# Tokens in another column order through all stages, with x1 and y stored row by row

## The chip, the cores and the metric

The kernel runs on one core of one Trainium2 chip. The metric is the device time of one execution in microseconds; less is better. Engines are named as in the profile: PE (TensorE matmuls), PEld (its weight loads), DVE (VectorE), ACT (ScalarE), POOL (GpSimd) and SP (SyncE, which here only issues DMAs). A DMA is split into pieces that are contiguous on both sides; the profile counts them as packets.

## What is computed

The input x is an image of 512 by 512 tokens with 128 channels, in fp32. Two layers follow one another, each added to its input. `_gn` normalises groups of 4 channels over the whole image.

```python
# layer 0: x = x + L0(_gn(x))
a = sigmoid((x @ Wa1 + ba1) * (x @ Wa2 + ba2))        # 16 channels
b = sigmoid((x @ Wb1 + bb1) * (x @ Wb2 + bb2))
g = sigmoid(x @ Wg + bg)
z = einsum('bikc,bkjc->bijc', a, b)
return g * (_ln(z) @ Wz + bz)
# layer 1: x = x + L1(_gn(x))
xn = layernorm(x)
h = linear(xn, pi) * sigmoid(linear(xn, gi)) * mask[..., None]
a1, b1, a2, b2 = split(h, 4, axis=-1)                 # 32 channels each
x1 = einsum('bikd,bjkd->bijd', a1, b1)
x2 = einsum('bkid,bkjd->bijd', a2, b2)
yn = layernorm(concatenate([x1, x2]))
return linear(yn, po) * sigmoid(linear(yn, go))
```

## The kernel before

The program has seven stages with a barrier between them. Tensors go through DRAM from one to the next: a_d, b_d, z_d, x1_d, h_d, y_d, r_d. Every engine's order is written out by hand with semaphores; no scheduler is at work.

- **Stage 1** (to 430 us) reads x in pieces of 64 KB and gathers statistics.
- **Stage 2** (`stage2_gates`, 430 to 1250 us) reads x in 256 loads of 8 rows by 128 columns (line 341: 128 partitions, one per column, 8 pieces of 512 B each), transposes to channels on partitions (line 353), projects and stores a_d and b_d in blocks of 128 tokens. A load waits for the slot to be transposed; there are four slots.
- **Stage 3** (`stage3_triangle`, to 1713 us) makes 16 channels of z for 128 rows at a time and stores z_d, channel by row by column, in four DMAs of 4 MB from POOL's queue (line 597).
- **Stage 4** (`stage4_layer0`, 1713 to 2640 us) goes row by row through the image, 16 rows to a loop pass in four groups of four. For a row, PE transposes four blocks of 128 tokens (line 680), multiplies z (line 688) and the gate (line 690), ACT makes the sigmoid (line 716), DVE mixes (line 749), POOL adds (line 783). SP's queue does for each group, in this order: the store of four rows of x1 (line 649, 1 MB), two loads of x (line 640, 512 KB each) and two of z (line 644, the same 32 channels to two places). x1_d has the channel as its first dimension, so a partition's four rows are one piece of 8 KB and partitions are 1 MB apart. x is read with `(i q p) c -> p i q c`: partition p takes the tokens p, 128+p, 256+p and 384+p of a row, four pieces of 512 B.
- **Stage 5** (`stage5_project`, to 4785 us) works on 16 regions of 128 by 128 tokens of x1_d, read in pieces of 512 B, and stores h_d. The mask comes into mask_n with one DMA (line 841); PE turns it (line 1066) and DVE keeps it (line 961) before the first tokens.
- **Stage 6** (`stage6_triangles`, to 5517 us) makes the 64 channels of y, each from 48 products (line 1196), and stores one channel of y_d at a time, 1 MB, from POOL's queue (line 1240). y_d has the channel first, so this megabyte is contiguous. Its last steps store r_d, the scale of each token.
- **Stage 7** (`stage7_layer1`, 5517 to 6609 us) goes through rows again. SP loads for four rows y (two DMAs of 64 partitions, line 1339) and r_d (line 1341), and for two rows x1 (line 1343). PE spreads the scale (line 1355), DVE scales (line 1403), ACT rounds (line 1449), DVE makes the rest (line 1407), PE projects (lines 1359 to 1361), ACT makes the gate (line 1454), DVE mixes (line 1413), POOL adds x1 (line 1484), PE transposes back (line 1375), ACT copies out (line 1438) and issues the store of two rows (line 1442), in pieces of 512 B.

Which token of a row stands in which column is free as long as all stages agree, since the products sum over all tokens of a row or column.

## Time and profile before

| | us |
|---|---|
| median of 3 runs | 6601.09 |
| lowest and highest | 6581.02, 6617.51 |
| profiled execution | 6610.76 |
| span of its instructions | 6609.1 |
| PE / DVE / ACT / POOL busy | 5324.7 / 4933.3 / 3568.5 / 2397.8 |

The span is the time from the first to the last instruction. The mean granted TensorE clock is 0.929 of full speed. The 16 DMA engines moved 1521.58 MB, 230 GB/s in the mean; 1461952 of the 1673897 packets are under 2 KB. Shares of the whole span mix stages with different limits, so what follows is read stage by stage.

### The profile page before, as it was taken

The numbers are of one execution on the slowest core, as the hardware profiler recorded it, in microseconds if no ns is written. First come the engines' busy times: TensorE is split into PE (matmuls) and PEld (weight loads), VectorE is DVE, ScalarE is ACT, GpSimd is POOL, SyncE is SP. The second block draws the span as 40 slices with busy tenths as digits, with TensorE's granted clock in tenths as the row PEclk, the third lists the DMA queues.
The fourth block names the chain that finished last, engine by engine and source line by source line (L and its number), as shares of the span: only waits on it lengthen the run. The fifth ranks groups of instructions, "written<-read, shape, count | busy, mean of one in ns | idle before, by whom it ended". The sixth has DMA issues, their size and how long they took to land. (4 is left out here: it accounts for less than half of the span.)

```text
span 6609.1 us, 113036 instructions
## 1 busy us (share of the span) xinstructions
PE 5324.7 (81%) x31445; PEld 3093.9 (47%) x31445; DVE 4933.3 (75%) x8646; ACT 3568.5 (54%) x5390; POOL 2397.8 (36%) x1756
## 2 busy tenths in 40 slices
PE   0026766755588888899999999999899996999999
PEld 0025655522355554555555555555544443445454
DVE  6887877465777778677777777777778886777776
ACT  0037888522566666444434443444367774777776
POOL 0014444200477776223322332333200003656665
PEclk9998888877799999899989998999899998999999
DMA  8967777765799999454455445544588886999999
GB/s 306 369 224 204 211 204 208 254 236 209 225 337 327 329 335 302 111 138 118 118 140 137 118 118 141 135 118 118 153 316 303 303 277 203 310 311 316 313 319 297
DMA packets 1673897, 1521.58 MB, mean 230 GB/s; under 512 B 42752, under 2 KB 1461952, under 8 KB 1655232
## 3 DMA queue, kind: packets, MB, share of 16 engines
q1 hardware_dynamic: 1319536, 1265.61, 62.2%
q10 hardware_dynamic: 332288, 167.79, 8.9%
q0 software_dynamic: 21840, 85.46, 3.2%
q8 instruction: 98, 1.61, 0.1%
q14 instruction: 135, 1.11, 0.1%
HBM read 997.04 MB, written 521.67 MB: 230 GB/s over the span
## 5 line engine op out<-in xcount | busy, mean ns | idle before, releaser
L915 ACT ACTIVATE s_gate<-s_g_ps,k_gi_bias 128x512 f32<-128x512 f32 x512 | 351.7, 687 | 1059.8 <-PE s_g_ps L1103 1059.8
L927 POOL TENSOR_TENSOR s_rstd<-s_var,k_minus_half 128x16 f32<-128x16 f32 x130 | 377.1, 2901 | 1495.1 <-DVE s_var L983 1495.1
L1484 POOL TENSOR_TENSOR s_oT<-s_gated,s_x1t 128x512 f32<-128x512 f32 x512 | 650.6, 1271 | 442.1 <-DVE s_gated L1413 435.7
L783 POOL TENSOR_TENSOR s_x1T<-s_gz,s_xT 128x512 f32<-128x512 f32 x512 | 650.0, 1269 | 254.4 <-DVE s_gz L749 252.8
L1196 PE MATMUL s_y_ps<-s_ab 128*128 128x512 f16 x3072 | 665.0, 380 | 36.0 <-DVE s_ab L1259 36.0
L395 POOL TENSOR_TENSOR s_low<-s_xh,s_high 128x512 f16<-128x512 f32 x256 | 383.4, 1498 | 849.0 <-DVE s_high L391 849.0
L1103 PE MATMUL s_g_ps<-s_xc,k_Wgi 128*128 128x512 f32 x1024 | 593.7, 662 | 0.0
L1005 DVE TENSOR_TENSOR s_xc<-s_xh,s_rstd_ps 128x512 f32<-128x512 f32 x513 | 352.6, 687 | 265.5 <-PE s_rstd_ps L1097 215.5
L749 DVE SCALAR_TENSOR_TENSOR s_gz<-s_z_ps,k_z_bias,s_g 128x512 f32<-128x512 f32 x512 | 384.5, 751 | 213.0 <-ACT s_g L716 210.7
L1106 PE MATMUL s_p_ps<-s_xc,k_Wpi 128*128 128x512 f32 x1024 | 535.7, 605 | 0.0
L690 PE MATMUL s_g_ps<-s_xT,s_Wg 128*128 128x512 f32 x1024 | 523.6, 593 | 0.0
L1012 DVE SCALAR_TENSOR_TENSOR s_h<-s_p_ps,k_pi_bias,s_gate 128x512 f32<-128x512 f32 x512 | 384.0, 750 | 152.7 <-PE s_p_ps L1106 149.0
L1196 PEld LDWEIGHTS s_y_ps<-s_ab 128*128 128x128 f16 x3072 | 301.0, 98 | 399.7 <-issue 38.6
L1454 ACT ACTIVATE s_gate<-s_g_ps,k_go_bias 128x512 f32<-128x512 f32 x512 | 352.0, 687 | 228.0 <-PE s_g_ps L1361 219.9
L969 DVE BATCH_NORM_STATS2 s_stats<-s_x_ps 128x6 f32<-128x128 f32 x2080 | 469.0, 283 | 5.4 <-PE s_x_ps L1083 5.4
L716 ACT ACTIVATE s_g<-s_g_ps,s_bg 128x512 f32<-128x512 f32 x512 | 351.8, 687 | 192.2 <-PE s_g_ps L690 192.2
L680 PEld LDWEIGHTS s_x_ps<-k_ident,s_xt 128*128 128x128 f32 x2048 | 247.3, 142 | 408.9 <-issue 241.4
L893 ACT ACTIVATE s_xh<-s_xg,k_gn_shift,k_gn_scale 128x512 f32<-128x512 f32 x524 | 420.5, 804 | 24.7 <-DMA s_xg<-x_d 24.5
L1407 DVE TENSOR_TENSOR s_low<-s_yn,s_high 128x512 f16<-128x512 f32 x256 | 267.5, 1045 | 222.9 <-ACT s_high L1449 222.9
L680 PE MATMUL s_x_ps<-k_ident,s_xt 128*128 128x128 f32 x2048 | 315.3, 277 | 103.7 <-DMA s_xt<-in_x 97.2
L412 ACT ACTIVATE s_xh<-s_turned_ps,k_gn_shift,k_gn_scale 128x512 f32<-128x512 f32 x512 | 373.7, 783 | 39.1 <-PE s_turned_ps L353 33.6
L364 PE MATMUL s_proj_ps<-k_Wab_high,s_high 128*128 128x64 f16 x2048 | 243.9, 197 | 180.4 <-DVE s_pre L481 172.6
(209 smaller groups left out, 12723.1 us busy)
## 6 DMA issues: line engine op xcount, KB each, us to landing
s_xt<-in_x SPq DMA_DIRECT2D x512, 512.0 KB, 6.6
s_xg<-x_d SPq DMA_DIRECT2D x264, 512.0 KB, 5.7
x_d<-s_x1T SPq DMA_DIRECT2D x128, 1024.0 KB, 6.3
h_d<-s_out SPq DMA_DIRECT2D x128, 1024.0 KB, 8.1
s_x1t<-x_d SPq DMA_DIRECT2D x256, 512.0 KB, 6.7
out<-s_ot ACTq DMA_DIRECT2D x256, 512.0 KB, 7.5
s_bt<-b_d SPq DMA_DIRECT2D x64, 1024.0 KB, 7.8
s_at<-h_d SPq DMA_DIRECT2D x64, 1024.0 KB, 4.9
```

The lines of the kernel that those rows point to most:

```text
L395: engine.tensor_tensor(low[:, u % 8, :], xh[:, u % 4, :], high[:, u % 8, :], ALU.subtract).then_inc(rest_ready[u % 2], 1)
L680: last = pe.transpose(x_ps[:, i % 4, q * P:(q + 1) * P], xt[:, i // U, i % U, q, :], K.ident[:])
L690: pe.matmul(g_ps[:, i % 2, 0:N], Wg[:], xT[:, i % 8, :], start=True, stop=True).then_inc(g_prod, 1)
L749: dve.scalar_tensor_tensor(gz[:, i % 4, :], z_ps[:, i % 2, 0:N], K.z_bias[:], g[:, i % 2, :], ALU.add, ALU.mult).then_inc(mixed, 1)
L783: pool.tensor_tensor(x1T[:, i // U, i % U, :], gz[:, i % 4, :], xT[:, i % 8, :], ALU.add).then_inc(added, 1)
L893: act.activation(xh[:, unit // 4 % 4, 4 * (unit % 4):4 * (unit % 4) + 4, :], src, ACT.Identity, bias=K.gn_shift[:], scale=K.gn_scale[:]).t ...
L969: last = dve.bn_stats(stats[:, 4 * (unit % 4) + r, :], x_ps[:, unit % 2, r * P:(r + 1) * P])
L1012: dve.scalar_tensor_tensor(h[:, 4 * unit:4 * unit + 4, :].rearrange("p r j -> p (r j)"), p_ps[:, unit % 2, :], K.pi_bias[:], gate[:, unit ...
L1103: pe.matmul(g_ps[:], K.Wgi[:], xc[:, unit % 2, :], start=True, stop=True).then_inc(g_done, 1)
L1106: pe.matmul(p_ps[:, unit % 2, :], K.Wpi[:], xc[:, unit % 2, :], start=True, stop=True).then_inc(p_done, 1)
L1196: last = pe.matmul(y_ps[:, n % 8, 0:N], ab[:, u % 2, 0, a, kb, ib * P:(ib + 1) * P], ab[:, u % 2, 1, b, kb, :], start=m == 0, stop=m == le ...
L1484: pool.tensor_tensor(oT[:, row % 4, :], gated[:, row % 2, :], x1t[:, row // 2, row % 2, :], ALU.add).then_inc(added, 1)
```

## The change

The column order changes from `(q p)` to `(p q)`: block q of a row now holds the tokens 4p+q, so the four tokens of a partition are neighbours, 2 KB in x and in the output. Rows go into blocks the same way (i = 4m+b) where a block of 128 rows is on the partitions: stage 2 reads rows 4 apart, stages 3 and 6 store their 128 rows 4 apart, stage 5 reads them so. x1_d becomes row by channel by column and y_d likewise, so one row of x1 is 256 KB in one piece and one channel of y is spread over the whole of y_d. Pieces: x loads of stage 4 and output stores of stage 7 from 512 B to 2 KB; x1 stores from 8 KB to 2 KB; x1 loads of stage 7 from 4 KB to 2 KB; the others keep their size. The mask is loaded into the tile h first, and one copy on DVE puts its columns in the new order. Stage 7 loads y with one DMA instead of two.

```diff
--- before.py
+++ after.py
@@ -304,7 +304,7 @@
     ROWS, UNITS = 8, 64
     PAIRS = UNITS // 2
     LAG = 4
-    x_v = x.rearrange("(rb n r j) c -> rb n j r c", rb=RB, r=ROWS, j=N)
+    x_v = x.rearrange("(n r b p q) c -> b q n p r c", r=ROWS, b=RB, p=P, q=RB)
     with ExitStack() as stack:
         s = Scope(nc, stack, "s2")
         xt = s.sbuf("xt", [P, 4, ROWS, P])
@@ -337,7 +337,7 @@
                         for n in range(32):
 
                             sp.wait_ge(turned, r * UNITS + (2 * n + 2))
-                            src = x_v[bass.ds(rb, 1), n % 16, bass.ds((c2 * 2 + n // 16) * P, P)].rearrange("a j r c -> (a j) r c")
+                            src = x_v[bass.ds(rb, 1), bass.ds(c2 * 2 + n // 16, 1), n % 16].rearrange("a e p r c -> (a e p) r c")
                             sp.dma_start(xt[:, n % 4, :, :], src).then_inc(loaded[n % 4], 16)
 
             @block.tensor
@@ -500,6 +500,7 @@
 
 
     RB, C, SLOTS = N // P, 16, 4
+    z_v = z_d.rearrange("c (p b) j -> b p c j", b=RB)
     with ExitStack() as stack:
         s = Scope(nc, stack, "s3")
         at = s.sbuf("at", [P, SLOTS, RB, P])
@@ -594,7 +595,7 @@
                 pool.sem_inc(left, 1)
                 with pool.Fori(0, RB) as ib:
                     pool.wait_ge(z_split, ib * 2 + 2)
-                    pool.dma_start(z_d[:, bass.ds(ib * P, P), :].rearrange("c i j -> i c j"),
+                    pool.dma_start(z_v[bass.ds(ib, 1)].rearrange("a p c j -> (a p) c j"),
                                    parts[:].rearrange("p h c j -> p (h c) j")).then_inc(stored, 16)
                     pool.wait_ge(stored, ib * 16 + 16)
                     pool.sem_inc(left, 1)
@@ -606,7 +607,7 @@
 
     CB, ROWS, U = N // P, 16, 4
     GROUPS = ROWS // U
-    x_v = x.rearrange("(i q p) c -> p i q c", q=CB, p=P)
+    x_v = x.rearrange("(i p q) c -> p i q c", q=CB, p=P)
     with ExitStack() as stack:
         s = Scope(nc, stack, "s4")
         xt = s.sbuf("xt", [P, GROUPS, U, CB, P])
@@ -646,7 +647,7 @@
                 def group(r, n, last=False):
 
                     sp.wait_ge(added, r * ROWS + (U * n + U + 8))
-                    sp.dma_start(x1_d[:, bass.ds(r * ROWS + U * n, U), :], x1T[:, n, :, :]).then_inc(stored[n], 16)
+                    sp.dma_start(x1_d[bass.ds(r * ROWS + U * n, U)].rearrange("i p j -> p i j"), x1T[:, n, :, :]).then_inc(stored[n], 16)
                     if not last:
                         sp.wait_ge(turned, r * ROWS + (U * n + U))
                         load_x(r + 1, n)
@@ -794,6 +795,7 @@
 
     RB, GROUPS = N // P, 8
     last_region = RB * RB
+    x1_v = x1_d.rearrange("(m b) p j -> b p m j", b=RB)
     with ExitStack() as stack:
         s = Scope(nc, stack, "s5")
         xg = s.sbuf("xg", [P, 2, 8, P])
@@ -802,6 +804,7 @@
         gate = s.sbuf("gate", [P, 2, BANK])
         h = s.sbuf("h", [P, P, P])
         rows_out = s.sbuf("rows_out", [P, 2, BANK])
+        mask_raw = h[:, 0:RB * N // P, :].rearrange("m (b k) c -> m b (k c)", b=RB)
         out1 = s.sbuf("out1", [P, 64, P])
         out2 = s.sbuf("out2", [P, 64, P])
         mask_n = s.sbuf("mask_n", [P, RB, N])
@@ -822,7 +825,7 @@
             return (t_ps if n % 4 < 2 else p_ps)[:, n % 2, :]
 
         loaded = s.sems("loaded", 2)
-        mask_loaded, mask_turned, mask_kept = [s.sem(n) for n in ("mask_loaded", "mask_turned", "mask_kept")]
+        mask_loaded, mask_parted, mask_turned, mask_kept = [s.sem(n) for n in ("mask_loaded", "mask_parted", "mask_turned", "mask_kept")]
         normed, x_turned, counted, var_ready, rstd_ready, parts_ready, parts_turned, rows_ready, chain = [
             s.sem(n) for n in ("normed", "x_turned", "counted", "var_ready", "rstd_ready", "parts_ready", "parts_turned", "rows_ready", "chain")]
 
@@ -838,13 +841,13 @@
         def _(block):
             @block.sync
             def _(sp):
-                sp.dma_start(mask_n[:], mask.rearrange("(b p) j -> p b j", p=P)).then_inc(mask_loaded, 16)
+                sp.dma_start(mask_raw, mask.rearrange("(p b) j -> p b j", b=RB)).then_inc(mask_loaded, 16)
 
                 def load(g, n):
 
                     place = g % last_region
                     sp.wait_ge(normed, g * 32 + (2 * n + 1))
-                    src = x1_d[:, bass.ds(place // RB * P + 8 * n, 8), bass.ds(place % RB * P, P)]
+                    src = x1_v[bass.ds(place // RB, 1), :, 8 * n:8 * n + 8, bass.ds(place % RB * P, P)].rearrange("a p m j -> (a p) m j")
                     sp.dma_start(xg[:, n % 2, :, :], src).then_inc(loaded[n % 2], 16)
 
                 def store(g, t, out, part):
@@ -952,6 +955,10 @@
 
             @block.vector
             def _(dve):
+                dve.wait_ge(mask_loaded, 16)
+                dve.tensor_copy(mask_n[:].rearrange("m b (q p) -> m b p q", q=RB),
+                                mask_raw.rearrange("m b (p q) -> m b p q", q=RB)).then_inc(mask_parted, 1)
+                dve.wait_ge(mask_parted, 1)
                 dve.sem_inc(scaled, 16)
                 dve.sem_inc(counted, 2)
                 dve.sem_inc(h_ready, 2)
@@ -1058,7 +1065,7 @@
             def _(pe):
                 pe.sem_inc(h_turned, 32)
 
-                pe.wait_ge(mask_loaded, 16)
+                pe.wait_ge(mask_parted, 1)
                 for cb in range(RB):
                     if cb >= 2:
                         pe.wait_ge(mask_kept, cb - 1)
@@ -1157,6 +1164,7 @@
 
 
     RB, D, SLOTS = N // P, 64, 4
+    y_v = y_d.rearrange("(p b) d j -> d p b j", b=RB)
     with ExitStack() as stack:
         s = Scope(nc, stack, "s6")
         at, bt = s.sbuf("at", [P, SLOTS, RB, N]), s.sbuf("bt", [P, SLOTS, RB, N])
@@ -1237,12 +1245,12 @@
                 with pool.Fori(0, D // GROUP) as r:
                     for u in range(GROUP):
                         pool.wait_ge(copied, r * (GROUP * RB) + ((u + 1) * RB + 8))
-                        pool.dma_start(y_d[bass.ds(r * GROUP + u, 1)].rearrange("a (b p) j -> p (a b) j", p=P),
+                        pool.dma_start(y_v[bass.ds(r * GROUP + u, 1)].rearrange("a p b j -> (a p) b j"),
                                        y[:, u, :, :]).then_inc(stored, 16)
                         pool.wait_ge(stored, r * (GROUP * 16) + (u + 1) * 16)
                         pool.sem_inc(left, 1)
                 pool.wait_ge(parts_ready, 1)
-                pool.dma_start(r_d.rearrange("(b p) k j -> p b k j", p=P), parts[:]).then_inc(parts_stored, 16)
+                pool.dma_start(r_d.rearrange("(p b) k j -> p b k j", b=RB), parts[:]).then_inc(parts_stored, 16)
                 pool.wait_ge(parts_stored, 16)
 
             @block.vector
@@ -1303,9 +1311,9 @@
 
 
     CB, PAIRS = N // P, 4
-    y_v = y_d.rearrange("d (r e) j -> e d r j", e=2)
+    y_v = y_d.rearrange("(r e) d j -> (e d) r j", e=2)
     r_v = r_d.rearrange("(r e) k j -> (e k) r j", e=2)
-    out_v = out.rearrange("(i q p) c -> p i q c", q=CB, p=P)
+    out_v = out.rearrange("(i p q) c -> p i q c", q=CB, p=P)
     with ExitStack() as stack:
         s = Scope(nc, stack, "s7")
         yt = s.sbuf("yt", [P, 2, 2, N])
@@ -1335,12 +1343,10 @@
                     for n in range(PAIRS):
                         if n % 2 == 0:
                             sp.wait_ge(scaled, r * PAIRS + (n + 2))
-                            for e in range(2):
-                                sp.dma_start(yt[64 * e:64 * e + 64, n // 2, :, :],
-                                             y_v[e, :, bass.ds(r * PAIRS + n, 2), :]).then_inc(y_loaded[n // 2], 16)
+                            sp.dma_start(yt[:, n // 2, :, :], y_v[:, bass.ds(r * PAIRS + n, 2), :]).then_inc(y_loaded[n // 2], 16)
                             sp.dma_start(rt[:, n // 2, :, :], r_v[:, bass.ds(r * PAIRS + n, 2), :]).then_inc(y_loaded[n // 2], 16)
                         sp.wait_ge(added, r * ROWS + (2 * n + 2))
-                        sp.dma_start(x1t[:, n, :, :], x1_d[:, bass.ds(r * ROWS + 2 * n, 2), :]).then_inc(x_loaded[n], 16)
+                        sp.dma_start(x1t[:, n, :, :], x1_d[bass.ds(r * ROWS + 2 * n, 2)].rearrange("i p j -> p i j")).then_inc(x_loaded[n], 16)
 
             @block.tensor
             def _(pe):
@@ -1350,7 +1356,7 @@
                 def spread_scale(r, n):
                     r, n = r + n // PAIRS, n % PAIRS
                     if n % 2 == 0:
-                        pe.wait_ge(y_loaded[n // 2], r * 48 + 48)
+                        pe.wait_ge(y_loaded[n // 2], r * 32 + 32)
                     pe.wait_ge(scaled, r * PAIRS + (n + 4))
                     pe.matmul(r_ps[:, 0:N], K.halves[:], rt[:, n // 2, n % 2, :], start=True, stop=True).then_inc(spread, 1)
 
@@ -1496,9 +1502,9 @@
     a_d = nc.dram_tensor("a_d", [RB, P, 16, N], FP32, kind="Internal").ap()
     b_d = nc.dram_tensor("b_d", [RB, P, 16, N], FP32, kind="Internal").ap()
     z_d = nc.dram_tensor("z_d", [32, N, N], FP16, kind="Internal").ap()
-    x1_d = nc.dram_tensor("x1_d", [P, N, N], FP32, kind="Internal").ap()
+    x1_d = nc.dram_tensor("x1_d", [N, P, N], FP32, kind="Internal").ap()
     h_d = nc.dram_tensor("h_d", [2, RB, P, 64, N], FP32, kind="Internal").ap()
-    y_d = nc.dram_tensor("y_d", [64, N, N], FP32, kind="Internal").ap()
+    y_d = nc.dram_tensor("y_d", [N, 64, N], FP32, kind="Internal").ap()
     r_d = nc.dram_tensor("r_d", [N, 3, N], BF16, kind="Internal").ap()
     with ExitStack() as stack:
         s = Scope(nc, stack, "k")
```

On SyncE's queue, at the end of a pass of stage 7 (four rows), before:

```order
L1339 ISA [waits s7_scaled]
L1339 DMA s_yt<-y_d 64x2x512
L1339 ISA
L1339 DMA s_yt<-y_d 64x2x512
L1341 ISA
L1341 DMA s_rt<-r_d 6x2x512
L1342 ISA
L1343 ISA [waits s7_added]
L1343 DMA s_x1t<-x_d 128x1024
```

and with the change:

```order
L1346 ISA [waits s7_scaled]
L1346 DMA s_yt<-y_d 128x2x512
L1347 ISA
L1347 DMA s_rt<-r_d 6x2x512
L1348 ISA
L1349 ISA [waits s7_added]
L1349 DMA s_x1t<-x_d 128x2x512
```

One of the two y loads ahead of r_d is gone, and the x1 load has two runs of 512 elements to a partition in place of one of 1024.

On VectorE at the start of stage 5, before:

```order
L953 UNCONDITIONAL_BRANCH [waits barrier_Pool_Activation_PE_DVE_SP_release]
L961 COPY s_mask_t<-s_t_ps 128x512 [waits s5_mask_turned] x4
L969 BN_STATS s_stats<-s_x_ps 128x6 [waits s5_x_turned]
L969 BN_STATS s_stats<-s_x_ps 128x6 x3
L969 BN_STATS s_stats<-s_x_ps 128x6 [waits s5_x_turned]
```

and with the change:

```order
L956 UNCONDITIONAL_BRANCH [waits barrier_Pool_Activation_PE_DVE_SP_release]
L959 COPY s_mask_n<-s_h 128x4x128x4 [waits s5_mask_loaded]
L968 COPY s_mask_t<-s_t_ps 128x512 [waits s5_mask_parted,s5_mask_turned]
L968 COPY s_mask_t<-s_t_ps 128x512 [waits s5_mask_turned] x3
L976 BN_STATS s_stats<-s_x_ps 128x6 [waits s5_x_turned]
L976 BN_STATS s_stats<-s_x_ps 128x6 x3
```

The copy that puts the mask in order stands ahead of the four that keep the turned mask. On PE, ACT and POOL no instruction moves.

## Rows read from the trace of the kernel before

**Rows 1.** Busy by window: span, busy of PE, PEld, DVE, ACT, POOL; PE clock, DMA share, GB/s
```profile
600.00:1100.00 500.00, 345.21 (x5164) 305.87 (x5162) 386.40 (x622) 418.15 (x673) 234.24 (x156) 0.87 0.72 206
1850.00:2450.00 600.00, 527.99 (x2362) 312.28 (x2361) 454.87 (x674) 405.06 (x675) 427.79 (x337) 1.00 1.06 331
4950.00:5400.00 450.00, 450.00 (x2087) 204.02 (x2085) 387.16 (x175) 327.15 (x305) 32.36 (x43) 1.00 0.88 303
5700.00:6400.00 700.00, 666.15 (x3518) 349.86 (x3515) 509.78 (x670) 496.95 (x837) 424.86 (x335) 1.00 1.03 315
```

**Rows 2.** Instructions of a line, four lines: count, duration ns min/median/max, first and last start
```profile
L353 PE MATMUL s_turned_ps<-k_ident,s_xt x2048: 272/273/476, 436.1 to 1241.3; 128*128 128x128 f32 x187
...
L749 DVE SCALAR_TENSOR_TENSOR s_gz<-s_z_ps,k_z_bias,s_g x512: 750/751/753, 1726.8 to 2622.5; 128x512 f32<-128x512 f32 x171
...
L1196 PE MATMUL s_y_ps<-s_ab x3072: 379/379/634, 4807.8 to 5472.4; 128*128 128x512 f16 x192
...
L1413 DVE SCALAR_TENSOR_TENSOR s_gated<-s_p_ps,k_po_bias,s_gate x512: 736/740/751, 5528.9 to 6602.1; 128x512 f32<-128x512 f32 x171
```

**Rows 3.** Waits in stage 4, 1850 to 2450 us: us in total, times, longest
```profile
PE s_x_ps L680 <- DMA s_xt<-in_x: 72.0, 84, 1.6
```

**Rows 4.** VectorE in order of time in stage 4: start, length, instruction
```profile
2103.47 0.75 DVE L749 SCALAR_TENSOR_TENSOR s_gz<-s_z_ps,k_z_bias,s_g 128x512 f32<-128x512 f32 x1 [0.16 <-ACT s_g L716]
...
2104.98 0.75 DVE L749 SCALAR_TENSOR_TENSOR s_gz<-s_z_ps,k_z_bias,s_g 128x512 f32<-128x512 f32 x1 [0.16 <-ACT s_g L716]
...
2107.68 0.75 DVE L749 SCALAR_TENSOR_TENSOR s_gz<-s_z_ps,k_z_bias,s_g 128x512 f32<-128x512 f32 x1 [1.35 <-ACT s_g L716]
```

**Rows 5.** VectorE in order of time in stage 7, five of nine rows of line 1413
```profile
5828.36 0.74 DVE L1413 SCALAR_TENSOR_TENSOR s_gated<-s_p_ps,k_po_bias,s_gate 128x512 f32<-128x512 f32 x1
...
5836.42 0.74 DVE L1413 SCALAR_TENSOR_TENSOR s_gated<-s_p_ps,k_po_bias,s_gate 128x512 f32<-128x512 f32 x1
5839.06 0.74 DVE L1413 SCALAR_TENSOR_TENSOR s_gated<-s_p_ps,k_po_bias,s_gate 128x512 f32<-128x512 f32 x1
...
5842.95 0.74 DVE L1413 SCALAR_TENSOR_TENSOR s_gated<-s_p_ps,k_po_bias,s_gate 128x512 f32<-128x512 f32 x1
5845.78 0.74 DVE L1413 SCALAR_TENSOR_TENSOR s_gated<-s_p_ps,k_po_bias,s_gate 128x512 f32<-128x512 f32 x1
```

**Rows 6.** Busy by window, three windows with one kind of transfer; columns as in rows 1
```profile
4774.00:4782.00 8.00, 0.00 (x0) 0.00 (x0) 0.00 (x0) 0.00 (x0) 0.00 (x0) 0.50 1.14 346
4811.00:4817.00 6.00, 6.00 (x28) 2.70 (x27) 1.77 (x1) 1.19 (x2) 0.00 (x0) 0.97 1.05 409
2660.00:2678.00 18.00, 7.40 (x28) 4.58 (x27) 6.39 (x28) 6.61 (x10) 5.58 (x2) 0.50 0.97 129
```

**Rows 7.** DMA view of stage 4, 1850 to 2450 us: packets, then issues with landing times
```profile
DMA packets 195375, 198.58 MB, mean 331 GB/s; under 512 B 6736, under 2 KB 179231, under 8 KB 184607
...
s_xt<-in_x SPq DMA_DIRECT2D x168, 512.0 KB, 7.8
```

**Rows 8.** The DMA queue of SyncE in order of time, in stage 4
```profile
2105.05 3.83 SPq L644 DMA_DIRECT2D s_zt<-z_d  x2
```

**Rows 9.** The chain of waits in stage 7, near 6006 us: start, length, what
```profile
6006.17 7.60 DMA s_rt<-r_d
```

**Rows 10.** The DMA queue of SyncE in order of time, in stage 7
```profile
6004.56 1.43 SPq L1339 DMA_DIRECT2D s_yt<-y_d  x2
```

**Rows 11.** TensorE at the start of stage 5 in order of time; the groups of stage 6
```profile
2648.18 3.87 PE L1066 MATMUL s_t_ps<-k_ident,s_mask_n 128*128 128x128 f32 x16 [7.26 <-DMA s_mask_n<-in_mask]
...
L1268 DVE TENSOR_TENSOR s_total<-s_total,s_y 128x2048 f32<-128x2048 f32 x44 | 100.5, 2284 | 0.0
```

**Rows 12.** DMA issues of stage 2 (600 to 1100 us), stage 6 (4950 to 5400) and stage 3
```profile
s_xt<-in_x SPq DMA_DIRECT2D x157, 512.0 KB, 4.3
...
y_d<-s_y POOLq DMA_DIRECT2D x43, 1024.0 KB, 8.4
...
z_d<-s_parts POOLq DMA_DIRECT2D x4, 4096.0 KB, 16.8
```

## The prediction

> **What bounds the kernel now.** I read the page's slices first, then a table by window, since the change touches only how DRAM is laid out and the stages have different limits. The reader should see four kinds of stage there [rows 1]. In stage 2 the DMA engines are busy 0.72 of the time, in stage 6 0.88 beside a PE that is busy all of its 450 us at full clock: neither waits for DMA. In stages 4 and 7 the DMA share is 1.06 and 1.03: always a packet in flight. Stage 5 moves the fewest bytes per microsecond in the page's slices. So time is to be had in stages 4 and 7, and only there.
>
> How much is bounded by the work beside the DMAs. **Stage 4**: line 749 runs once a row, from 1726.8 to 2622.5 us, 895.7/511 = 1.753 us a row [rows 2]; inside the stage it is 600/337 = 1.78. PE waits for x loads, 72 us in this window [rows 3]. Where it doesn't, line 749 returns after 1.51 us (2103.47 to 2104.98); at every group of four comes a gap of 2.7 (2104.98 to 2107.68) [rows 4]. 1.51 is PE's own floor; at it the stage would be 511 x (1.753 - 1.51) = 124 us shorter. **Stage 7**: (6602.1 - 5528.9)/511 = 2.100 us a row [rows 2]. Its rhythm without a DMA wait is 8.06 us for four rows (5828.36 to 5836.42); where the load of y and r_d is late, one interval grows from 1.3 or 1.6 to 2.83 (5842.95 to 5845.78), about every eighth row [rows 5]. The rhythm alternates 1.3 to 1.6 and 2.6 us and belongs to the ring of ACT, DVE, PE and POOL (gate, mix, round, rest). The next four rows took 9.36, and would take 8.14 with a 1.61 in place of the 2.83, so the floor is some 2.03 a row, and removing every DMA wait is worth 511 x (2.100 - 2.03) = 36 us, however full the DMA share looks.
>
> **The change, part by part.** *Price of a piece.* Three windows show one kind of transfer each [rows 6]: stores of h_d in 512 B pieces run at 346 GB/s, loads of h_d in 2 KB pieces at 409. The third, 512 B pieces of x1_d, comes below. So 512 B to 2 KB is worth 15% of the time of those bytes. The Trainium skill (DMA: Bandwidth & Descriptors, Specifications) gives 512 B as the smallest transfer that runs at line rate; by that nothing would be gained by going to 2 KB, and these two windows disagree with it.
>
> *Stage 4.* A row moves 262 KB of x, 262 KB of x1 and 66 KB of z. The packets under 2 KB in the window are the x loads: 168 loads of 1024 pieces [rows 7]. Before: x 262/346 = 0.758, x1 in 8 KB pieces at no more than the 409 of 2 KB taken for it 0.641, z 0.160, together 1.559 us; the measured row is 1.78, 1.14 times that. After: 0.641 + 0.641 + 0.160 = 1.442 us, a saving of 0.117, or 60 us over the stage. That is my lower end, since it assumes the loss of 0.22 a row stays; 8 KB pieces may have been a little cheaper than 2 KB, which the rest of the range covers. The upper end is the floor, 124 us. Something of the loss should go too: SP's queue is held 3.83 us at the two small z loads behind two x loads of 1024 pieces each [rows 8], the x1 store waits behind them, and a group then issues 512 + 512 + 64 pieces in place of 2048 + 128 + 64. I take a row of 1.58, near the middle: 511 x 0.173 = 88 us. At 1.58 DMA and PE are nearly equal; where x stops being late, PE is late next.
>
> *Stage 7.* A row's DMA work by the same prices: x1 0.641, y 0.320, output 0.758, 1.73 us with r_d before, 1.61 after, both under 2.03. The engines are thus not short of rate; the wait is one of latency: r_d lands 7.60 us after its issue [rows 9], at the back of the two y loads that hold the queue 1.43 us [rows 10]. After it, one y issue is gone (some 0.7 us earlier), the output needs a quarter of the packets, and x1's go from 128 to 256 a load at 0 to 0.02 us a row. The waits come to 8 x 0.07 = 0.56 us in eight rows, less than the issue that goes, so most vanish: 30 of the 36 us, ends 0 and 36.
>
> *Stage 5.* The new copy moves 2048 elements a partition on DVE. Nearest: 2284 ns for a tensor_tensor of 2048; the mask is waited for 7.26 us by PE and all that follows starts behind it [rows 11]. Nothing covers the copy: cost 3 us, ends 2 (no slowdown by its stride) and 5. Region loads keep 512 B pieces and are waited for only at the start, so a gain there is taken as nothing.
>
> *Stages 2, 3 and 6: no piece changes size, only its address.* Stage 2's x loads go from contiguous 64 KB to 512 B out of every 2 KB. They land in 4.3 us [rows 12], the period of a load is (1241.3 - 436.1)/256 = 3.15 us [rows 2], four slots deep, so some 8 us of lateness is covered. Cost nothing, up to 10 us. The z store's 1 KB pieces were 512 KB apart by channel and stay so. Stage 6's y store goes from contiguous to 2 KB pieces 128 KB apart; a channel takes (5472.4 - 4807.8)/64 = 10.38 us [rows 2], its loads 5.13 and the store 2.56 at 409 GB/s, leaving 2.7 us of slack, and the store has four slots against a landing of 8.4 us [rows 12]. Cost nothing.
>
> **Sum**: 88 + 30 - 3 = 115 us. The profiled execution has 6610.8 us, so 6495.8; it lies 9.7 above the median of the runs, 6601.1, and against that the forecast is 6486. Its own range, 6450 to 6530, comes from stage 4 at 60 to 120 and stage 7 at 15 to 36. A measurement here tells from no change what exceeds 0.5%, 33 us.
>
> **The rivals.** *1. Both stages reach their floors.* 124 + 36 - 3 = 157 us, 6444. For it: 1.442 is under 1.51, and the reads of 2 KB lost nothing at share 1.05. Against: 2% to 5% of slack is little for reads and writes mixed, and stage 4 now reaches only 1.78 against 1.559. The Trainium skill (same page, Latency and other measured facts) reports copies slowing as rows lie 512 KB to 8 MB apart; x1_d has 1 MB between partitions before and none after, so by that the loss would go with the layout. Chance 0.18.
>
> *2. Small pieces are no limit in the mixed stages.* The 1.78 is then the price of turning between loads and stores, and 8 KB stores cut into four lose what the x loads win: stage 4 gives 0, stage 7 its 15 to 30 through the shorter queue, less 3: 6580. For it: 331 GB/s in stage 4 is below even the 346 of pure 512 B pieces. Against: the 15% seen in pure windows. This is also where the skill's line-rate rule would lead. Chance 0.12.
>
> *3. Slower, by stage 2's loads.* In the third window of [rows 6], 512 B pieces out of 2 KB rows that lie 1 MB apart come at 129 GB/s with a share of 0.97, a third of the usual. Stage 2 takes that pattern over (eight rows 1 MB apart to a partition). It needs 524 KB every 3.15 us, 166 GB/s. Below this the loads decide: at 129 a load takes 4.06 us, 256 x 0.91 = 233 us more, and 6486 becomes 6719. The sign turns at 146 GB/s (115/256 = 0.45 us a load). Against: there the partitions, and with them all 16 engines, were 1 MB apart, while here neighbouring partitions are 2 KB apart. Chance 0.08.
>
> *4. The y store becomes the bound of stage 6.* Its partitions lie 512 KB apart. Until it takes 2.56 + 2.7 = 5.3 us (200 GB/s) it costs nothing. At 165 GB/s it takes 6.35, 64 x 1.1 = 70 us more: 6556. Against: the z store with 512 KB between channels lands 4 MB in 16.8 us [rows 12], 250 GB/s with its latency. By the skill's section just named, 512 KB apart gives 207 GB/s, just within the slack. Chance 0.10.
>
> **How the numbers follow.** Forecast 0.52, the rivals 0.18, 0.12, 0.08 and 0.10. Range 6430 to 6570: it holds the forecast's own range, rival 1 with the 15 us by which runs differ, and most of rival 4. Over 0.5% faster (below 6568): 0.52 + 0.18 + a third of rival 2 + most of rival 4 = 0.82; within 0.5%: the rest of these, 0.10; slower: rival 3, 0.08.
>
> **What would show it.** Stage 4's DVE row at 1.51 to 1.65 us with the gap at every fourth row smaller, x waits of PE well under 72 us in 600, and packets of 2 KB. Stage 7's row at 2.03 to 2.06, few waits for r_d. Stages 2 and 6 as long as before, with shares of 0.72 and 0.88 rising a little. PE's first work in stage 5 about 3 us later behind the mask. Wrong: a stage 4 still at 1.75; line 353 or 1196 spread over more than 805 or 665 us; or a stage 7 row clearly below 2.0, which would mean that its rhythm was made by DMA after all.

## The result, and the profile after

The changed kernel is a little slower: 6640.9 us median (6637.4 to 6664.5) against 6603.2 (6581.0 to 6617.5), ratio 1.0066 with a 95% interval of 1.0046 to 1.0086. The profiled execution has a span of 6638.9 us, 29.8 more than before.

The lines that mark the stages, in the kernel after (count, duration in ns, first and last start). Four answer to [rows 2]; line 1012, DVE's scaling, marks stage 5:

```profile
L353 PE MATMUL s_turned_ps<-k_ident,s_xt x2048: 272/273/474, 440.9 to 1379.3; 128*128 128x128 f32 x187
...
L750 DVE SCALAR_TENSOR_TENSOR s_gz<-s_z_ps,k_z_bias,s_g x512: 749/751/753, 1860.6 to 2694.4; 128x512 f32<-128x512 f32 x171
...
L1012 DVE TENSOR_TENSOR s_xc<-s_xh,s_rstd_ps x513: 675/689/690, 2740.2 to 4819.8; 128x512 f32<-128x512 f32 x171
...
L1204 PE MATMUL s_y_ps<-s_ab x3072: 379/379/631, 4877.6 to 5543.3; 128*128 128x512 f16 x192
...
L1419 DVE SCALAR_TENSOR_TENSOR s_gated<-s_p_ps,k_po_bias,s_gate x512: 735/744/752, 5597.6 to 6632.2; 128x512 f32<-128x512 f32 x171
```

and the line of stage 5 in the kernel before:

```profile
L1005 DVE TENSOR_TENSOR s_xc<-s_xh,s_rstd_ps x513: 677/687/690, 2674.2 to 4749.8; 128x512 f32<-128x512 f32 x171
```

Last start minus first gives each stage's length, with the others before from [rows 2]:

| stage | before | after | difference |
|---|---|---|---|
| 2 | 805.2 | 938.4 | +133.2 |
| 4 | 895.7 | 833.8 | -61.9 |
| 5 | 2075.6 | 2079.6 | +4.0 |
| 6 | 664.6 | 665.7 | +1.1 |
| 7 | 1073.2 | 1034.6 | -38.6 |
| between and outside them | | | -8.0 |

Stages 4 and 7 gained 100 us together, and stage 2 lost more. The table by window, of the kernel after (span, busy of PE, PEld, DVE, ACT, POOL; PE clock, DMA share, GB/s), answers to [rows 1]:

```profile
600.00:1100.00 500.00, 306.87 (x4492) 277.59 (x4488) 370.71 (x547) 375.00 (x587) 186.32 (x137) 0.88 0.81 179
1970.00:2570.00 600.00, 575.06 (x2575) 340.39 (x2573) 496.51 (x736) 441.87 (x736) 468.54 (x368) 1.00 1.05 361
5020.00:5470.00 450.00, 450.00 (x2087) 204.02 (x2085) 387.12 (x175) 328.18 (x305) 30.67 (x43) 1.00 0.89 304
5760.00:6460.00 700.00, 687.78 (x3630) 357.68 (x3629) 522.80 (x692) 509.53 (x865) 439.61 (x346) 1.00 0.97 325
```

Stage 4 moves 361 GB/s in place of 331, stage 7 325 in place of 315. Stage 2 moves less, 179 in place of 206, at a higher DMA share, 0.81 in place of 0.72: every byte there costs more DMA time. Its loads, and who waited for them, first in the DMA view of 600 to 1100 us, then in the waits of the same window, then a window of stage 2 in which loads of x ran almost alone:

```profile
s_xt<-in_x SPq DMA_DIRECT2D x137, 512.0 KB, 11.1
```
```profile
PE s_turned_ps L353 <- DMA s_xt<-in_x: 123.6, 89, 3.9
```
```profile
896.00:914.00 18.00, 10.71 (x149) 9.89 (x150) 12.72 (x19) 9.85 (x15) 4.46 (x4) 0.71 0.79 152
```

A load lands 11.1 us after its issue in place of 4.3 [rows 12], and PE waits 123.6 us of 500; before, its transposes waited for x only once in the whole stage, 6.3 us. In the window where x came almost alone the loads ran at 152 GB/s. Over the whole stage, with the stores of a and b beside them, they ran slower: 256 loads of 524 KB in 938.4 us are 143 GB/s, one load every 3.67 us. To last 805 us the stage needs 166.

### The profile page after: what moved, and what is told of

It reads as the page before. It is cut to its first block and busy times, and to the rows that moved or that the text cites. A ratio compares the mean times of both kernels' runs of the same rounds, so it can differ in the third digit from the quotient of the medians.

```text
span 6638.9 us, 112638 instructions
## 1 busy us (share of the span) xinstructions
PE 5344.8 (81%) x31445; PEld 3119.1 (47%) x31445; DVE 4992.6 (75%) x8647; ACT 3584.5 (54%) x5390; POOL 2363.1 (36%) x1756
## 5 line engine op out<-in xcount | busy, mean ns | idle before, releaser
L395 POOL TENSOR_TENSOR s_low<-s_xh,s_high 128x512 f16<-128x512 f32 x256 | 348.1, 1360 | 1022.6 <-DVE s_high L391 1022.6
L353 PE MATMUL s_turned_ps<-k_ident,s_xt 128*128 128x128 f32 x2048 | 371.8, 314 | 280.7 <-DMA s_xt<-in_x 242.8
L353 PEld LDWEIGHTS s_turned_ps<-k_ident,s_xt 128*128 128x128 f32 x2048 | 255.8, 159 | 307.8 <-issue 193.7
```

The source lines that it names most:

```text
L353: last = pe.transpose(turned_ps[:, u % 4, k * P:(k + 1) * P], xt[:, u // 2 % 4, 4 * (u % 2) + k, :], K.ident[:])
```

## Experiments

In most of these kernels one stage alone reads its tokens in another order, and every stage does its full work. Such a kernel doesn't compute the reference's output; g1_split, e6_x1 and f1_pairs do. Where only one stage's loads differ, that stage's length is the reading; where no interval is given, the whole time is one run.

**Which part of the new pattern is slow.** The change gave stage 2's loads two new steps: columns 2 KB apart, and rows 1 MB apart. One alone each:

```diff
 (e1_columns, in the kernel before)
-    x_v = x.rearrange("(rb n r j) c -> rb n j r c", rb=RB, r=ROWS, j=N)
+    x_v = x.rearrange("(b n r p q) c -> b q n p r c", r=ROWS, b=RB, p=P, q=RB)
 (e2_rows, in the kernel before)
+    x_v = x.rearrange("(n r b q p) c -> b q n p r c", r=ROWS, b=RB, p=P, q=RB)
 ... (in both, the load takes its block from x_v as the changed kernel does)
```

> The kernel before, whose stage 2 alone loads x in the new column order (every fourth token, a partition's pieces of 512 B lie 2 KB from its neighbour's) with its eight rows still next to each other, 256 KB apart. Tokens are then in another order in stage 2 than in the rest, so the output is not the reference's; the amount of work is the same. Stage 2's line 353 spans 805 us before and 938 after the change. Theory A (pieces of 512 B that lie alone in 2 KB are what is slow): 930 to 940 here, whole kernel near 6735. Theory B (eight rows 1 MB apart in a partition are slow): 800 to 810, whole kernel near 6600. Theory C (both are needed): between 805 and 850.

> The kernel before, whose stage 2 alone takes every fourth row (a partition's eight pieces are 1 MB apart) with columns contiguous, so each row of a load is one stretch of 64 KB. Rows are in another order in stage 2 than in the rest, so the output is not the reference's. Theory A: line 353 spans 800 to 810 us, whole kernel near 6600. Theory B: 930 to 940, whole kernel near 6735. Theory C: between 805 and 850.

Line 353 in the first:

```profile
L353 PE MATMUL s_turned_ps<-k_ident,s_xt x2048: 272/273/477, 433.2 to 1240.6; 128*128 128x128 f32 x187
```

and in the second:

```profile
L353 PE MATMUL s_turned_ps<-k_ident,s_xt x2048: 272/273/477, 437.3 to 1244.5; 128*128 128x128 f32 x187
```

Both span 807 us, with 7.1 and 6.5 us of waiting for x (6.3 in the kernel before), and their loads land in 4.0 and 4.4 us (600 to 1100 us). Theories A and B fall; each step alone is free and the two together cost 133 us (the whole kernels took 6607.7 and 6625.6 us; the second's excess stands in its stage 4, 921.5 us, which it doesn't touch).

**Whether stage 2's loads are all of the loss.** The changed kernel with those loads as before, and with its loads cut into pieces of 1 KB:

```diff
 (e3_back, in the changed kernel)
+    x_v = x.rearrange("(rb n r j) c -> rb n j r c", rb=RB, r=ROWS, j=N)
 (e4_1kb, in the changed kernel)
+    x_v = x.rearrange("(n r b p h w) c -> b h n p r w c", r=ROWS // 2, b=RB, p=P, h=2, w=2)
+    src = x_v[bass.ds(rb, 1), bass.ds(c2, 1), n].rearrange("a e p r w c -> (a e p) r (w c)")
 ... (the tile's side of the load is written to match; e3_back takes its source as the kernel before)
```

> The changed kernel with the x loads of stage 2 alone as before. Stage 2 then has another token order than the rest, so the output is not the reference's. If the loss is all in those loads, line 353 spans 805 us and the kernel takes 6640.9 - 133 = 6508 us (6495 to 6520): the gain of stages 4 and 7 is then 62 + 39 us as their traces say, less 4. If part of stage 2's loss comes from elsewhere (the state the chip is in, later stages), it stays above 6530.

> The changed kernel with stage 2's 512 KB loads cut otherwise: 4 rows by 2 neighbouring tokens a partition, 1 KB pieces that lie alone in 2 KB, rows still 1 MB apart. Same bytes, each read once, but they land in another order, so the output is not the reference's. Theory A: each access fetches more of what it opens, loads speed up clearly: line 353 back to 800 to 830 us, kernel 6508 to 6535. Theory B (the 1 MB between rows): four jumps in place of eight for the same bytes, so half of the loss stays, 850 to 880. If what limits is none of the two, 930 to 940.

Line 353 in e3_back, then in e4_1kb:

```profile
L353 PE MATMUL s_turned_ps<-k_ident,s_xt x2048: 272/273/477, 436.2 to 1242.2; 128*128 128x128 f32 x187
```
```profile
L353 PE MATMUL s_turned_ps<-k_ident,s_xt x2048: 272/273/477, 434.7 to 1243.4; 128*128 128x128 f32 x187
```

e3_back took 6508.3 us (6483.2 to 6514.1), ratio 0.9826 (0.9795 to 0.9858), inside the range set for it, and its stage 2 spans 806.0 us: nothing but those loads turned the change's gain into a loss. That the median falls on the forecast microsecond is luck, since its runs lie up to 31 us apart. e4_1kb took 6497.6, ratio 0.9821 (0.9797 to 0.9845); its stage 2 spans 808.7 us, so pieces of 1 KB are as good a cure as the old order.

**How large the steps must be.** Rows 512 KB apart with columns 2 KB apart (e7_rows2), and rows 1 MB apart with columns 1 KB apart (g2_cols2), both with 512 B pieces:

```diff
 (e7_rows2, in the changed kernel)
+    x_v = x.rearrange("(f n r b p q) c -> f b q n p r c", f=2, r=ROWS, b=2, p=P, q=RB)
 (g2_cols2, in the changed kernel)
+    x_v = x.rearrange("(n r b h p w) c -> b h w n p r c", r=ROWS, b=RB, h=2, p=P, w=2)
 ... (in both, the load's indices are written to match)
```

> The changed kernel whose stage 2 takes every second row in place of every fourth: a partition's eight pieces of 512 B lie 512 KB apart in place of 1 MB, columns still 2 KB apart. Rows are in another order than in the rest, so the output is not the reference's. The eight rows 256 KB apart cost nothing and 1 MB apart cost 133 us. If the loss grows with the step, line 353 spans 850 to 890 us; if only steps of 1 MB and more hurt, 805; if everything above 256 KB does, 930 to 940.

> The changed kernel whose stage 2 takes every second token in place of every fourth: pieces of 512 B, 1 KB from the neighbouring partition's, the eight rows still 1 MB apart. Tokens are in another order than in the rest, so the output is not the reference's. Rows 1 MB apart with contiguous columns cost nothing (line 353 at 807 us), with columns 2 KB apart 133 us. If it takes the full 2 KB step, 805 to 815 us; if the loss grows with the step, 850 to 890; under theory D, where the rows decide once columns are not contiguous, 930.

Line 353 in the first, then in the second:

```profile
L353 PE MATMUL s_turned_ps<-k_ident,s_xt x2048: 272/273/476, 436.7 to 1241.8; 128*128 128x128 f32 x187
```
```profile
L353 PE MATMUL s_turned_ps<-k_ident,s_xt x2048: 272/273/477, 434.2 to 1243.1; 128*128 128x128 f32 x187
```

805.1 and 808.9 us: halving either step removes the whole loss. The length of the stage can't tell more than that, since a load that comes late within its slots costs nothing. Landing tells more: 5.0 us in both (600 to 1100 us), against 4.3 in the kernel before and 11.1 in the changed one. So the stage takes these loads at full pace, but they are not quite as quick as before.

**Whether a single load is at fault.** First each load split into two of four rows:

```diff
 (g1_split, in the changed kernel)
-                            sp.dma_start(xt[:, n % 4, :, :], src).then_inc(loaded[n % 4], 16)
+                            for h in (0, 4):
+                                sp.dma_start(xt[:, n % 4, h:h + 4, :], src[:, :, :, h:h + 4, :]...).then_inc(loaded[n % 4], 16)
```

> The changed kernel whose stage 2 issues each 512 KB load as two of 4 rows (same 512 B pieces, same places, every 1 KB of tile the same). Theory D (what hurts is how many rows 1 MB apart are fetched for one partition in a row, eight; the 1 KB version has four): line 353 back to 805 to 830 us and the kernel near 6510 to 6530. Theory E (what hurts is that only a quarter of each row's bytes is touched by all requests in flight, whatever the cut): 930 to 940 stays, kernel near 6640. SyncE issues twice as many loads of some 0.37 us, 190 us in 805, which should hide.

6644.2 us, ratio 1.0038 (1.0025 to 1.0050). Line 354, where the transposes stand in this kernel:

```profile
L354 PE MATMUL s_turned_ps<-k_ident,s_xt x2048: 272/273/475, 436.3 to 1377.3; 128*128 128x128 f32 x187
```

941.0 us: theory D falls; the cut of a load does not matter. Then the very same loads, every one with its 512 B pieces, rows 1 MB and columns 2 KB apart, in another order of issue:

```diff
 (h1_altcol, in the changed kernel)
-src = x_v[bass.ds(rb, 1), bass.ds(c2 * 2 + n // 16, 1), n % 16]...
+src = x_v[bass.ds(rb, 1), bass.ds(c2 * 2 + n % 2, 1), n // 2]...
 (h2_altrow, in the changed kernel)
+src = x_v[bass.ds(rb // 2 * 2 + n % 2, 1), bass.ds(c2 * 2 + n // 16, 1), bass.ds(rb % 2 * 8 + n % 16 // 2, 1)]...
```

> The changed kernel whose stage 2 issues the very same 512 KB loads (512 B pieces, 2 KB apart, rows 1 MB apart) in another order: odd loads take the neighbouring column block, so that the loads in flight together touch both halves of every 1 KB. Tokens land in other places, so the output is not the reference's. If what is slow belongs to a single load (its pieces, their jumps), line 353 stays at 930 to 940 us. If it is the set of addresses that all loads in flight at a time share, it falls back clearly, to 805 to 850.

> As the one before, but odd loads take the neighbouring row block: all loads in flight stay on the same quarter of every 2 KB and together touch two rows of every four. Tokens land in other places, so the output is not the reference's. By the set of addresses in flight: line 353 at 805 to 850 us, as the version with rows 512 KB apart was at 805. By the single load: 930 to 940.

Line 353 in h1_altcol:

```profile
L353 PE MATMUL s_turned_ps<-k_ident,s_xt x2048: 272/273/477, 438.6 to 1247.3; 128*128 128x128 f32 x187
```

and in h2_altrow:

```profile
L353 PE MATMUL s_turned_ps<-k_ident,s_xt x2048: 272/273/477, 438.0 to 1242.1; 128*128 128x128 f32 x187
```

808.7 and 804.1 us; the kernels took 6508.0 and 6508.2. The DMA view of h1_altcol from 600 to 1100 us:

```profile
s_xt<-in_x SPq DMA_DIRECT2D x154, 512.0 KB, 5.9
```

In h2_altrow the median is 5.9 us too, against 11.1 for the same loads in the order of the change. This settles the place of the fault: the loss isn't that of a single load. A run of loads is slow when all that are in flight stay on the same quarter of every 2 KB and on the same row of every four; mixing either with its neighbour brings the stage back to its full pace. That a few memory channels then take all the traffic would explain this, but no run shows the channels.

Stage 5 of the changed kernel shows the same from another side. Its x1 loads have the very pattern of stage 2's: 512 B pieces, 2 KB apart from partition to partition, the eight rows 1 MB apart. But there are two slots in place of four, and DMA moves only some 130 GB/s in all from 3000 to 4000 us. They land in 4.3 us over the whole kernel; in e6_x1 (below), whose eight rows are neighbours, in 3.7:

```profile
s_xg<-x_d SPq DMA_DIRECT2D x264, 512.0 KB, 4.3
```
```profile
s_xg<-x_d SPq DMA_DIRECT2D x264, 512.0 KB, 3.7
```

So at this lower demand the pattern costs 0.6 us a load, which only the start of the stage can feel: ACT waits for these loads four times there, 7.0 us in all, and not later.

**What stages 4 and 7 gained from.** The kernel before, with stage 4's x loads alone in 2 KB pieces, and with x1's layout alone:

```diff
 (e5_x4, stage 4 of the kernel before)
-    x_v = x.rearrange("(i q p) c -> p i q c", q=CB, p=P)
+    x_v = x.rearrange("(i p q) c -> p i q c", q=CB, p=P)
 (e6_x1, kernel before, with its store and both loads to match)
-    x1_d = nc.dram_tensor("x1_d", [P, N, N], FP32, kind="Internal").ap()
+    x1_d = nc.dram_tensor("x1_d", [N, P, N], FP32, kind="Internal").ap()
```

> The kernel before, whose stage 4 alone loads x in the new order (2 KB pieces); x1 is still stored in 8 KB pieces 1 MB apart, and stage 7 writes its 512 B pieces as before. Tokens are in another order in stage 4 than elsewhere, so the output is not the reference's. Theory P (what stage 4 gained is the price of 512 B pieces): line 749 spans 830 to 840 us in place of 896. Theory Q (it gained from x1 losing its 1 MB steps): 890 to 896. Theory R (both): between, 850 to 880.

> The kernel before with x1 laid out row by channel by column in DRAM and nothing else: its stores go from 8 KB to 2 KB pieces, its loads in stage 7 from 4 KB to 2 KB, its stage 5 loads keep 512 B. Theory P: stage 4 unchanged or slower, line 749 at 895 to 915 us; stage 7 (line 1413) at 1073 or a little more. Theory Q: line 749 at 835 to 850. Stage 5's first region loads, which stood at 129 GB/s with 1 MB between partitions, tell besides whether that arrangement was what slowed them.

The marks of stages 4 and 7 in e5_x4:

```profile
L749 DVE SCALAR_TENSOR_TENSOR s_gz<-s_z_ps,k_z_bias,s_g x512: 749/751/754, 1726.8 to 2551.9; 128x512 f32<-128x512 f32 x171
```
```profile
L1413 DVE SCALAR_TENSOR_TENSOR s_gated<-s_p_ps,k_po_bias,s_gate x512: 735/740/751, 5456.1 to 6521.6; 128x512 f32<-128x512 f32 x171
```

and in e6_x1:

```profile
L749 DVE SCALAR_TENSOR_TENSOR s_gz<-s_z_ps,k_z_bias,s_g x512: 749/751/753, 1728.3 to 2589.2; 128x512 f32<-128x512 f32 x171
```
```profile
L1413 DVE SCALAR_TENSOR_TENSOR s_gated<-s_p_ps,k_po_bias,s_gate x512: 736/740/752, 5488.6 to 6527.2; 128x512 f32<-128x512 f32 x171
```

Stage 4: 825.1 us by the x pieces, 860.9 by x1's layout, 833.8 with both. Unedited, the same stage differs by up to 26 us between runs of one code (895.7, 898.2 and 921.5 with the old loads and layout; 821.3 to 847.1 in nine with the new). Both single readings lie below every old one, so both edits gain; but e5_x4 lies among those with both, so x1's layout adds nothing that can be seen once x comes in 2 KB pieces. x1's layout gains although its store pieces shrink from 8 KB to 2 KB, so theory P alone falls; 860.9 is short of what theory Q had set as well. Stage 7: 1065.5 and 1038.6 us, with the change 1034.6; kernels with all of the old layout have 1062.6 to 1073.2. Nearly all of its gain is x1's layout; neither the 2 KB output pieces nor the single y load were needed for it.

The first x1 loads of stage 5 tell the same. In e6_x1, from 2620 to 2634 us, the window that answers to the third of [rows 6]:

```profile
2620.00:2634.00 14.00, 8.11 (x37) 6.09 (x36) 8.84 (x45) 6.71 (x10) 2.94 (x1) 0.50 0.72 204
```

204 GB/s in 512 B pieces at a DMA share of 0.72, where 1 MB between partitions had given 129 at 0.97. In the page's DMA table the median landing goes from 5.7 to 3.7 us.

**A version that beats both.** The whole change, with stage 2 rebuilt for 1 KB pieces, so that every stage has the same order: a load takes four rows of two neighbouring tokens a partition, the two column blocks of a pass fill side by side, their tiles and b's output tile are held twice.

```diff
 (f1_pairs, in the changed kernel, with the turning of b and the stores to match)
-        ab = s.sbuf("ab", [P, 2, 32, P])
-        b_out = s.sbuf("b_out", [P, 16, P])
+        ab = s.sbuf("ab", [P, 2, 2, 32, P])
+        b_out = s.sbuf("b_out", [P, 2, 16, P])
...
-                            sp.dma_start(xt[:, n % 4, :, :], src).then_inc(loaded[n % 4], 16)
+                            sp.dma_start(xt[:, n % 4, :, :].rearrange("p (r w) c -> p r (w c)", w=2), src).then_inc(loaded[n % 4], 16)
...
-                    act.activation(ab[:, half, :, i0:i0 + 8], gate[:, q % 2, :, :].rearrange("p r c -> p c r"),
+                    act.activation(ab[:, c2, :, :, 4 * q:4 * q + 4], gate[:, q % 2, :, :].rearrange("p (r w) c -> p w c r", w=2),
```

> The changed kernel with stage 2 rebuilt around pieces of 1 KB: a load takes 4 rows of two neighbouring tokens a partition, so the two column blocks of a pass fill side by side; their tiles are held twice, and the turning of b of the first pass goes into the second. If the loads were all that was wrong, line 353 spans 800 to 815 us and the kernel takes 6495 to 6515 us. If the new order of turning b costs (two blocks at the end of four passes in place of one at the end of eight), some 10 to 30 us more. If stage 2 stays at 930, the short pieces were not the cause in the true kernel.

6511.5 us (6502.7 to 6528.2), ratio 0.9846 with an interval of 0.9823 to 0.9870. Its stage 2:

```profile
L353 PE MATMUL s_turned_ps<-k_ident,s_xt x2048: 272/273/477, 434.4 to 1250.2; 128*128 128x128 f32 x187
```

815.8 us, 11 more than before the change. With the same pieces e4_1kb had 808.7, so 7 of them lie in the rebuilt passes; the later turning of b is the likely place, but wasn't tried apart. The gain of stages 4 and 7 (827.1 and 1034.5 us) stays whole.

## Why the prediction was wrong

The forecast was 6486 us, and the kernel took 6640.9. Point by point, by the profiled executions:

- **Stage 2: the step that failed.** It said of the x loads that they land in 4.3 us with a period of 3.15, four slots deep, so "some 8 us of lateness is covered. Cost nothing, up to 10 us." Slots cover lateness, but no lack of rate: over the stage the loads fell to 143 GB/s, under the 166 that it needs, landing rose to 11.1 us, and the stage grew by 133.2 us. Rival 3 had this mechanism, its place and the sign turning at 146 GB/s, at a chance of 0.08 and a price of 233 us; the rate that it borrowed, 129 GB/s, was too low. Its counter-argument was that there the partitions were 1 MB apart and here only the rows. Rows 1 MB apart are indeed free by themselves (e2_rows), but the slow row of the trace before had both steps too, with their parts exchanged: 2 KB from row to row and 1 MB from partition to partition. That exchange didn't save stage 2, and on that row 0.08 was too little.
- **Stage 4: right in kind, smaller in size.** The sum of piece prices gave 60 us, the floor 124, and I took 88; 61.9 came. (Between the runs with the old and the new layout it is 49 to 100 us, so the size is less sure than it looks.) The term that was too large is "something of the loss should go too". Its sign did show in SyncE's queue, where the two z loads hold it 1.22 us now:

```profile
2105.66 1.22 SPq L645 DMA_DIRECT2D s_zt<-z_d  x2
```

  instead of 3.83 [rows 8]. Yet the row came to 833.8/511 = 1.632 us, 1.13 times its sum of prices, as 1.753 had been 1.12 times before, so by this reading nothing of the loss beyond the price of pieces went. (The prediction's 1.14 set the 1.78 of a window against the sum, and took its saving from the 1.753 of the stage.) In e6_x1 the z loads still hold the queue 3.3 to 3.5 us between 2090 and 2122 us, and the stage gains all the same; the release of the queue wasn't tried apart. The wait for x was also read too small: 72.0 us [rows 3] is what the transposes waited, while their weight loads waited besides

```profile
PEld s_x_ps L680 <- DMA s_xt<-in_x: 103.1, 63, 2.2
```

  and with the change, from 1970 to 2570 us, the two are

```profile
PEld s_x_ps L681 <- DMA s_xt<-in_x: 74.1, 69, 1.5
```
```profile
PE s_x_ps L681 <- DMA s_xt<-in_x: 23.7, 72, 0.7
```

  so x is still late, and the floor of 1.51 isn't reached. The price of a piece itself came from stores in 512 B pieces (346 GB/s) and loads in 2 KB pieces (409), which mixes direction with size; e5_x4, with loads on both sides, gained 71 us where the price gave 60. And 8 KB and 2 KB pieces of x1 were priced alike, which left no room for what x1's layout does by itself.
- **Stage 7: right in the number, by luck in part.** 30 us were forecast out of 36, and 38.6 came. The row takes 1034.6/511 = 2.025 us, the floor read from its rhythm (2.03), and line 1419 returns in that rhythm, 6000.18, 6001.52, 6004.08, 6005.67 and again 6008.32. The wait was the one named: PE waits for r_d 51 times in the stage before and twice after. But the reason given, one y issue less and fewer output packets, was not the one: e6_x1 had neither, there the wait came 13 times, and it reached 1038.6. Landing of the x1 loads went from 6.7 to 5.5 us there (5700 to 6400 us). The 0 to 0.02 us a row that the prediction set for their doubled pieces stood on no row; they came faster instead.
- **Stage 5: nearly right.** The mask copy takes 2.02 us:

```profile
2719.71 2.02 DVE L959 COPY s_mask_n<-s_h 128x2048 f32<-128x2048 f32 x1 [5.55 <-DMA s_h<-in_mask]
```

  It was priced at 3. From stage 4's last mix to the first scaling of stage 5 it takes 45.8 us where it took 51.7; in e6_x1, with x1's layout and no copy, 45.2. So the layout gave more than the copy took, a gain that the prediction took as nothing. Inside the stage 4.0 us are lost. They are real, since the nine kernels that have the change in this stage take 2079.0 to 2079.7 us and the five without it 2074.7 to 2076.3, but their cause stays open; e6_x1 has 2075.4 us, so x1's layout isn't it.
- **Stage 6: right.** The y store, now 512 KB between partitions, lands in 8.5 us as against 8.4 and costs nothing, so rival 4 fell.
- **Rival 1 and rival 2** fell as well: neither did stage 4 reach its floor, nor was it free of the price of pieces (e5_x4 alone gains 71 us).

Without the loss of stage 2 the change would have gained 100 us (e3_back against the kernel before), where 115 were forecast.

## What to carry to other kernels

In this kernel a transfer's price was its size, its pieces and the set of addresses that all transfers in flight shared; a new order that improves the pieces of one stage can put every load of another at the same place within two steps, here 2 KB and 1 MB. So judge a change of layout stage by stage by the rate each stage needs and not by its slots, and where a pattern runs slow anywhere in the trace, give it a real chance wherever the change takes it, also with the parts of its steps exchanged. The cure may be small: take two neighbours in one piece (f1_pairs), or only alternate neighbouring blocks in the order of issue (seen in h1_altcol and h2_altrow, not built into a kernel whose stages all keep one order).

## What the runs showed that I had not expected

- Loads of 512 B pieces with 1 MB between rows and 2 KB between columns: each step alone costs the stage nothing (807.2 and 807.4 us), both together 133 us, half of either nothing (805.1 and 808.9), and the same loads issued alternately nothing (808.7 and 804.1). They land in 4.4 and 4.0, 11.1, twice 5.0, and twice 5.9 us. The Trainium skill (DMA: Bandwidth & Descriptors, Latency and other measured facts) has copies slowing with a row pitch of 512 KB to 8 MB, and suspects channels hit in step; there the pitch lies between partitions and the copies go from memory to memory. Here 1 MB between a partition's rows is free by itself, and loads of x1 in 512 B pieces with 1 MB between partitions ran at 129 GB/s, so the pitch alone doesn't tell.
- Stores of x1 in 2 KB pieces that lie together were better for stage 4 than 8 KB pieces 1 MB apart while x came in 512 B pieces: 860.9 us in one run against 895.7 to 921.5. Beside x in 2 KB pieces no difference shows.
- A stage can show a DMA share above 1 and be within 4% of its engines' own rhythm: stage 7 had 1.03 at 2.100 us a row, and is at 2.025 with 0.97.
